# Gated cross-attention and expert FFN on one core: keys projected once, split high and low, and repeated by DMA through a DRAM scratch, with 96-row score operands and a new order of the turn

## What is computed

```python
q, k, v = split_heads(ln(x) @ Wq.T + bq), split_heads(ctx @ Wk.T + bk), split_heads(ctx @ Wv.T + bv)
scores = einsum('bhqd,bhkd->bhqk', q, k) / sqrt(8)
scores = where(mask, finfo.min, scores)
x = x + tanh(g_xattn) * (merge(softmax(scores) @ v) @ Wo.T + bo)
n = ln(x)
w = softmax(n @ Wg + bg) - sigmoid(n @ Wt + bt) / 8, negatives set to 0, normalised over the experts
x = x + tanh(g_ffn) * sum_e w_e * (gelu(n @ W1_e + b1_e) @ W2_e + b2_e)
```

## Time and profile before

| | us |
|---|---|
| median of 3 runs | 683.03 |
| profiled execution, whole | 685.3 |
| its span | 683.5 |
| first T10 (group 0) | 34.20 |
| T10 of group 14 | 265.47 |
| T10 of group 15 | 280.44 |
| last product of the attention phase ends | 297.4 |
| TensorE busy | 633.4 (93%) |
| VectorE busy | 532.4 (78%) |
| ScalarE busy | 432.8 (63%) |
| GpSimd busy | 188.4 (28%) |
| mean granted TensorE clock | 0.98 |

### The profile page before, as it was taken

The page is one execution under the profiler, slowest core; times in us unless marked ns, Lnnn a source line. Parts: engine busy times, 40 slices in busy tenths (PEclk is TensorE's granted clock), DMA queues, the critical chain, the costliest instruction groups (busy, mean ns, idle before and its releaser), DMA issues.

```text
span 683.5 us, 14449 instructions
## 1 busy us (share of the span) xinstructions
PE 633.4 (93%) x3944; PEld 478.2 (70%) x3944; DVE 532.4 (78%) x1083; ACT 432.8 (63%) x764; POOL 188.4 (28%) x242
## 2 busy tenths in 40 slices
PE   2899999999999999739999999999999999999996
PEld 2566666666666766427878878778788788787784
DVE  5778888899988888346877877868778778788686
ACT  3456666666666666418767757667576677675773
POOL 6224444444444443100230221212302202213022
PEclk9999999999999999959999999999999999999999
DMA  6544444444444444103121111111211211111110
GB/s 190 140 110 121 109 120 119 114 114 116 111 111 111 114 110 114 40 0 85 47 62 43 51 47 56 51 34 64 70 35 46 61 46 46 46 61 53 54 46 15
DMA packets 37386, 52.74 MB, mean 77 GB/s; under 512 B 9328, under 2 KB 20464, under 8 KB 37360
## 3 DMA queue, kind: packets, MB, share of 16 engines
q1 hardware_dynamic: 37360, 52.42, 27.8%
HBM read 26.58 MB, written 2.23 MB: 42 GB/s over the span
## 4 chain that ended last, share of the span: by engine, by line
PE 79%; DVE 8%; POOL 3%; DMA 3%; issue 2%; SPq 2%; ACT 2%; DVEq 0%; POOLq 0%; ACTq 0%
PE ps_y L1041 8%; PE ps_y L1043 8%; PE ps_y L1042 8%; PE ps_h L1061 8%; PE ps_h L1063 8%; PE ps_h L1062 8%; PE scores L994 5%; PE scores L995 4%; PE scores L1002 3%; PE scores L1003 3%; POOL yT L527 3%; DVE neg_max L654 3%; PE heads L1013 3%; PE misc L882 2%; PE misc L883 2%
## 5 line engine op out<-in xcount | busy, mean ns | idle before, releaser
L627 ACT ACTIVATE h_sb<-ps_h,b_sb 128x512 f32<-128x512 f32 x256 | 175.4, 689 | 116.2 <-PE ps_h L1063 103.6
L841 DVE TENSOR_TENSOR h_low<-h_sb,h_high 128x512 fp32r<-128x512 f32 x256 | 164.4, 682 | 0.0
L527 POOL TENSOR_TENSOR yT<-yT,weighted 128x512 f32<-128x512 f32 x56 | 72.3, 1292 | 309.2 <-DVE weighted L829 308.4
L837 DVE CAST h_high<-h_sb 128x512 fp32r<-128x512 f32 x128 | 86.8, 678 | 81.8 <-ACT h_sb L627 81.8
L1041 PE MATMUL ps_y<-h_high,w_high 128*128 128x512 f32 x256 | 102.2, 399 | 5.0 <-DVE h_low L841 5.0
L1061 PE MATMUL ps_h<-x_high,w_high 128*128 (+1 forms) x256 | 101.9, 398 | 0.1
L1043 PE MATMUL ps_y<-h_high,w_low 128*128 128x512 f32 x256 | 101.3, 396 | 0.0
L1042 PE MATMUL ps_y<-h_low,w_high 128*128 128x512 f32 x256 | 100.9, 394 | 0.0
L1063 PE MATMUL ps_h<-x_high,w_low 128*128 (+1 forms) x256 | 100.8, 394 | 0.0
L1062 PE MATMUL ps_h<-x_low,w_high 128*128 (+1 forms) x256 | 100.0, 391 | 0.0
L654 DVE TENSOR_REDUCE neg_max<-scores 128x4 f32<-128x512 f32 x128 | 83.6, 685 | 12.5 <-PE scores L1003 11.7
(11 more groups left out here) (122 smaller groups left out, 990.7 us busy)
## 6 DMA issues: line engine op xcount, KB each, us to landing
w_row<-w_scratch SPq DMA_DIRECT2D x64, 256.0 KB, 3.2
k_masked<-k_stack SPq DMA_DIRECT2D x64, 128.0 KB, 2.4
k_cur<-k_stack SPq DMA_DIRECT2D x16, 512.0 KB, 3.0
q_masked<-q_stack SPq DMA_DIRECT2D x64, 96.0 KB
w_raw<-in_w_ffn SPq DMA_DIRECT2D x16, 256.0 KB, 2.7
ctx_sb<-in_ctx SPq DMA_DIRECT2D x16, 128.0 KB, 2.1
out_y<-y_out SPq DMA_DIRECT2D x8, 256.0 KB, 3.6
probs<-in_wqk SPq DMA_DIRECT2D x2, 256.0 KB, 3.1
```

What stands on the lines that cost most here:

```text
L527: nc.gpsimd.tensor_tensor(yT[:], yT[:], weighted[:, e % 2, :], ALU.add).then_inc(added, 1)
L627: nc.scalar.activation(h_sb[:, j % HBUF, :], ps_h[:, j % 4, :], ACT.Gelu_apprx_tanh, bias=b1_sb[:, j:j + 1]).then_inc(h_done, 1)
L841: V.tensor_tensor(h_low[:, j % HBUF, :], h_sb[:, j % HBUF, :], h_high[:, j % HBUF, :].bitcast(F32), ALU.subtract).then_inc(low2_done, 1)
```

## The change

- Keys are projected once: three matmuls with 128 output rows, dense weights `wk_high` and `wk_low`. ScalarE adds the bias and rounds to `k_high`, VectorE leaves the rest in `k_low`. SyncE stores `k_high` twice and `k_low` once to a DRAM scratch `k_scratch` of 96 rows a group (`store`), and from there loads `k_cur` (96 rows, one DMA) and `k_masked` (four DMAs of 24 rows). `k_stack` goes, with four of the eight `part` and `stacks` steps of a turn.
- Queries stay threefold by matmuls, but with 96 instead of 128 output rows. The score operands have 96 rows (98 with the two rows of maxima).
- The pipeline is one turn deeper: inputs are turned in turn it for group it+3 (before it+2), heads, `merged` and `wo` follow one turn later, x2T and gate two turns.
- Biases come by twelve small DMAs that ScalarE issues at the start.
- All engines' orders are written anew. On TensorE `values(g, 0, 0)` and `values(g, 0, 1)` stand apart.

The diff, its core (lines of other moved steps are left out, and `part` and `stacks` of the queries, which only lose rows 96 to 127):

```diff
-BANKS = [["p45", "inputs", "x2T", "p01"],
-         ["p67", "max0", "p23"],
-         ["v", "heads", "merged", "gate", "wo"]]
-AHEAD = {"p45": 1, "p67": 1, "v": 1, "inputs": 2, "x2T": -1, "max0": 1, "heads": 0,
-         "p01": 2, "merged": 0, "p23": 2, "gate": -1, "wo": 0}
-FIRST, LAST = -3, NG
-STEADY = (2, NG - 3)
+BANKS = [["k", "x2T", "q01", "inputs"],
+         ["heads", "merged", "wo", "max0", "gate", "q23"],
+         ["v"]]
+AHEAD = {"k": 2, "x2T": -2, "q01": 2, "inputs": 3,
+         "heads": -1, "merged": -1, "wo": -1, "max0": 1, "gate": -2, "q23": 2, "v": 2}
+FIRST, LAST = -4, NG + 1
+STEADY = (2, NG - 4)
+KROWS = 3 * ROWS * HD
...
+        k_dram = nc.dram_tensor("k_scratch", (NG, KROWS, SLABS * GT), F32)
...
-                sp.dma_start(q_masked[24:26, :, :, b * S:(b + 1) * S].rearrange("p r s q -> p (r s) q").bitcast(F32),
+                sp.dma_start(q_masked[KROWS:KROWS + 2, :, :, b * S:(b + 1) * S].rearrange("p r s q -> p (r s) q").bitcast(F32),
                              maxT[:, b * S:(b + 1) * S].bitcast(F32)).then_inc(max_in[b], 16)
+            store_v = k_dram[:].rearrange("g (r c d) (s t) -> g c r (d s) t", r=ROWS, c=3, t=GT)
+            def store(c, src, g, done):
+                sp.dma_start(of_group(store_v, g)[:, c].rearrange("g r p t -> (g r) p t"), src[:].bitcast(F32)).then_inc(done, 16)
+            def load(dst, rows, g):
+                return sp.dma_start(dst.rearrange("p s t -> p (s t)").bitcast(F32), of_group(k_dram[:], g)[:, rows, :].rearrange("g p x -> (g p) x"))
             def body(it):
-                if (g := group_at(it, 0)) is not None:
-                    sp.wait_ge(maxT1_done, g + 1)
-                    settle(sp)
-                    max_rows(1)
-                if (g := group_at(it, 1)) is not None:
-                    misc_wait_read(sp, "p01", it - 1)
-                    settle(sp)
-                    misc_wait_read(sp, "p23", it - 1)
-                    settle(sp)
-                    if isinstance(g, int) and g == 0:
-                        sp.wait_ge(pad_done, 2)
+                if (g := group_at(it, 2)) is not None:
+                    sp.wait_ge(k_high_done, g + 1)
+                    settle(sp)
+                    store(0, k_high, g, high_stored)
+                    store(2, k_high, g, high_stored)
+                    misc_wait_read(sp, "k", g)
+                    settle(sp)
+                    store(1, k_low, g, low_stored)
+                if (g := group_at(it, 1)) is not None:
+                    sp.wait_ge(high_stored, g * 32 + 32)
+                    settle(sp)
+                    sp.wait_ge(low_stored, g * 16 + 16)
+                    settle(sp)
+                    if first(g):
+                        sp.wait_ge(pad_done, 3)
+                    else:
+                        sp.wait_ge(scoresT_full[1], fill_of(g - 1, GB - 1, SLABS - 1))
+                        settle(sp)
+                    load(k_cur[0:KROWS, :, :], slice(0, KROWS), g).then_inc(kcur_in, 16)
+                    misc_wait_read(sp, "q01", g)
+                    settle(sp)
+                    misc_wait_read(sp, "q23", g)
+                    settle(sp)
+                    for r in range(ROWS):
+                        rows = slice(3 * HD * r, 3 * HD * (r + 1))
+                        sp.dma_start(q_masked[rows, r, :, :].bitcast(F32), q_stack[rows, :, :].bitcast(F32)).then_inc(qm_in, 16)
+                    misc_wait_read(sp, "max0", g)
+                    settle(sp)
+                    max_rows(0)
+                if (g := group_at(it, 2)) is not None and not first(g):
+                    sp.wait_ge(masknxt_done, g)
+                    settle(sp)
+                    sp.wait_ge(maskcur_done, g)
+                    settle(sp)
+                    sp.dma_start(mask_words[:], of_group(mask_v, g)).then_inc(mask_in, 16)
+                if (g := group_at(it, 3)) is not None and not first(g):
+                    misc_wait_full(sp, "inputs", g - 1)
+                    settle(sp)
+                    sp.dma_start(ctx_sb[:], of_group(ctx_v, g).rearrange("g p b d -> (g p) b d")).then_inc(ctx_in, 16)
+                if (g := group_at(it, 2)) is not None:
+                    if not first(g):
+                        sp.wait_ge(wsplit_done, g)
+                        settle(sp)
+                        sp.dma_start(w_raw[:], of_group(a["w_ffn"], g).rearrange("g p x -> (g p) x")).then_inc(w_in, 16)
+                    sp.wait_ge(high_stored, g * 32 + 32)
+                    settle(sp)
+                    sp.wait_ge(low_stored, g * 16 + 16)
+                    settle(sp)
+                    if first(g):
+                        sp.wait_ge(pad_done, 3)
                     else:
                         sp.wait_ge(scoresN_full[1], fill_of(g - 1, GB - 1, SLABS - 1))
                         settle(sp)
                     for r in range(ROWS):
-                        rows = slice(32 * r, 32 * r + 32)
-                        sp.dma_start(k_masked[rows, r, :, :].bitcast(F32), k_stack[rows, :, :].bitcast(F32)).then_inc(km_in, 16)
-                if (g := group_at(it, 3)) is not None and not (isinstance(g, int) and g == 0):
-                    misc_wait_full(sp, "inputs", it)
-                    settle(sp)
-                    sp.dma_start(ctx_sb[:], ctx_v[g] if isinstance(g, int) else ctx_v[bass.ds(g, 1)]).then_inc(ctx_in, 16)
-                if (g := group_at(it, 1)) is not None:
-                    misc_wait_read(sp, "p45", it)
-                    settle(sp)
-                    misc_wait_read(sp, "p67", it)
-                    settle(sp)
-                    if not (isinstance(g, int) and g == 0):
-                        sp.wait_ge(scoresT_full[1], fill_of(g - 1, GB - 1, SLABS - 1))
-                        settle(sp)
-                    for r in range(ROWS):
-                        rows = slice(32 * r, 32 * r + 24)
-                        sp.dma_start(q_masked[rows, r, :, :].bitcast(F32), q_stack[rows, :, :].bitcast(F32)).then_inc(qm_in, 16)
-                    sp.dma_start(k_cur[:].bitcast(F32), k_stack[:].bitcast(F32)).then_inc(kcur_in, 16)
-                    misc_wait_read(sp, "max0", it)
-                    settle(sp)
-                    max_rows(0)
-                if (g := group_at(it, 2)) is not None and not (isinstance(g, int) and g == 0):
-                    sp.wait_ge(masknxt_done, g)
-                    settle(sp)
-                    sp.wait_ge(maskcur_done, g)
-                    settle(sp)
-                    sp.dma_start(mask_words[:], mask_v[g] if isinstance(g, int) else mask_v[bass.ds(g, 1)]).then_inc(mask_in, 16)
-                    sp.wait_ge(wsplit_done, g)
-                    settle(sp)
-                    sp.dma_start(w_raw[:], a["w_ffn"][g] if isinstance(g, int) else a["w_ffn"][bass.ds(g, 1)]).then_inc(w_in, 16)
+                        rows = slice(3 * HD * r, 3 * HD * (r + 1))
+                        load(k_masked[rows, r, :, :], rows, g).then_inc(km_in, 16)
+                if (g := group_at(it, 1)) is not None:
+                    sp.wait_ge(maxT1_done, g + 1)
+                    settle(sp)
+                    max_rows(1)
             loop(sp, body)
...
+            bias_v = a["bqk"].rearrange("(r c d) (n s) -> n r c d s", r=ROWS, c=COMBOS, s=SLABS)
+            for r in range(ROWS):
+                rows = slice(3 * HD * r, 3 * HD * (r + 1))
+                act.dma_start(bk[4 * HD * r:4 * HD * (r + 1), :], bias_v[0, r, 0]).then_inc(bias_in, 16)
+                act.dma_start(bq[rows, :], bias_v[1, r, 0:3].rearrange("c d s -> (c d) s")).then_inc(bias_in, 16)
+                act.dma_start(low_rows[rows, :], a["low_rows"][4 * HD * r:4 * HD * r + 3 * HD, SLABS:]).then_inc(bias_in, 16)
...
+                    misc_wait_full(act, "k", g)
+                    wait_count(act, high_stored, g * 32)
+                    nc.scalar.activation(k_high[:], misc[:, bank_of("k"), 0:GT], ACT.Identity, bias=bk[:]).then_inc(k_high_done, 1)
...
-                    k = bank_of(f"p{i}{i + 1}")
-                    dve.wait_ge(part_done, g * (2 * SLABS) + (i + 2))
-                    if i < SLABS:
-                        wait_count(dve, km_in, g * (ROWS * 16))
-                        wait_count(dve, kcur_in, g * 16)
-                    else:
-                        wait_count(dve, qm_in, g * (ROWS * 16))
-                    for j in (i, i + 1):
-                        dst = (k_stack if j < SLABS else q_stack)[:, j % SLABS, :]
-                        ins = nc.vector.scalar_tensor_tensor(dst, misc[:, k, (j - i) * GT:(j - i + 1) * GT], bqk[:, j:j + 1],
-                                                             part[:, j % 4, :].bitcast(F32), ALU.add, ALU.subtract)
-                    ins.then_inc(misc_read[k], 1)
-                if (g := group_at(it, 1)) is not None:
-                    stacks(2, g)
+                    what = f"q{i}{i + 1}"
+                    dve.wait_ge(part_done, g * SLABS + (i + 2))
```

(23 more changed lines are left out.)

502 lines of the change are left out of this document (264 added, 238 removed).

## The result

| | us |
|---|---|
| kernel before, median of 5 runs | 683.03 |
| changed kernel, median of 5 runs (688.07 to 691.30) | 690.13 |
| ratio, with its 95% interval | 1.0095 (1.0074 to 1.0115) |
| changed kernel, profiled execution, whole | 690.13 |
| its span | 688.4 |

The account below looks back on a forecast made before the run. TensorE sets the turn before the change (16.32 us); after it, SyncE's loop of 17.09 us was to decide. Start +4.9, middle +7.3, end -1.4 sum to +10.8: 694 us against 683.03, 1.6% slower, range 679 to 702.

Parts of the forecast that it names:

- the middle: Attention phase, T10 of group 0 to group 14: 14 turns of 17.09 us, 238.6 against 231.27, +7.3 us.
- a loop over SyncE: Steady turn: T10, T13, SyncE's issues from `k_cur` to `max_rows(1)`, its landing, next T10; one trip is 17.09 us.
- T13 to the issue of `k_cur`: Steady turn: from T13's start on TensorE to SyncE's first issue behind it, 0.92 us.
- `k_cur` to `max_rows(1)`, issuing: Steady turn: SyncE's issues and waits from `k_cur` until `max_rows(1)` is issued, 10.82 us.
- landing of `max_rows(1)`: Steady turn: from the start of its issue until the transfer that T10 needs has landed, 2.26 us.
- the price of the four loads from DRAM: SyncE's issue time for the four `k_masked` loads of 24 rows: 3.14 us, as for `q_masked` of the same shape.
- The stores cost nothing: Steady turn: stores fall between `max_rows(1)` and T13, with some 5 us there, so they cost nothing.
- TensorE at 15.5: TensorE's need in a steady turn after the change: 16.32 - 1.59 + 0.45 + 0.36 = 15.5 us.
- The start: Up to T10 of group 0: later ScalarE, stores and N00 at 24.8 move it from 34.20 to 39.1, +4.9 us.
- The end: T10 of group 14 to group 15: no `k_masked` load in the way, 13.6 against 14.97, -1.4 us.
- Rival 1: Steady turn: four DRAM loads cost 1.6, loop falls to 15.55, TensorE stays the bound; 669 us; chance 0.18.
- Rival 3: Steady turn: `max_rows(1)` lands after 3.0 us in place of 2.26, 15 turns add 11 us; 705 us; chance 0.08.

## Why the prediction was right, and where it was not

**Sign and range: right. Cause: wrong.** It placed +7.3 of +10.8 in the middle, as a loop over SyncE. The middle gave 1.3 back, and the loss was made before T10 of group 0.

**The loop, term by term.** It exists. Its terms, in turns at whose end T10 waits for `max_rows(1)` (of the changed kernel from 109.06, of the run with the SBUF source from 159.55):

| term | forecast | changed kernel | SBUF source |
|---|---|---|---|
| T13 to the issue of `k_cur` | 0.92 | 1.27 | 1.03 |
| `k_cur` to `max_rows(1)`, issuing | 10.82 | 9.42 | 10.57 |
| landing of `max_rows(1)` | 2.26 | 3.21 | 2.40 |
| T10 to T13 | 3.09 | 2.81 | 2.95 |
| together | 17.09 | 16.71 | 16.95 |

With the forecast's price the forecast's loop comes out, each term within 0.3 us. At the real price it sets only some turns: in the shown turn of 16.14 its landing found room, and TensorE's work and the gate's wait set the time.

The step that failed is the price of the four loads from DRAM: 3.14 was taken because "shape is what the rows differ by" (they differ by source too), 1.81 was measured, and the run with an SBUF source shows 3.08 at the same shape. The same error, smaller, is in `k_cur`: 0.53 against 0.34. The row that said so was there: `w_raw`, from DRAM, was the cheapest of the loads, and I put that down to its 128 rows. The Trainium skill ("DMA: Bandwidth & Descriptors", on why a DMA increments its semaphore by 16) was leaned on for the high price, since it has the sequencer write the increments of engines left out; by that the two loads of 24 rows would cost alike. The runs don't agree: 0.33 and 0.72 us by source (medians of 64 issues each).

**"The stores cost nothing": wrong, and this was the change's real cost.** In issuing they push `k_cur` by up to 0.24 us: it follows T13 by 1.04 where the store of `k_low` is issued half a us ahead of T13 (144.88 and 145.42, `k_cur` at 146.46), and by 1.27 or 1.28 where it is issued just behind T13. In the queues they run at a share of 0.23, and what stands behind them lands later (`k_cur` 5.6 against 3.6). The same section of the Trainium skill states the rule that I should have put against the change: the number of engines is the largest up to 16 that divides the slowest dimension of both sides, 4 for these stores, and "Rules for kernel authors" on the same page advises a multiple of 16 outermost. The traces agree with it as far as a share can: 0.23 with 4 outermost, 0.39 and twice the GB/s with 32. I used the rule for the loads and did not try it on the stores.

**TensorE at 15.5.** It was 15.62 busy, which bears the work of the sum out, and 0.44 of the gate's wait for the bank that it shares with the maxima. The wait was in the new order of the turn and I had not looked for one there. The 96- and 98-row operands take the 0.46 us a pair that was taken for them (T13 at 161.53 to its `natural` at 161.99).

**The start: +4.9, and it was +7.76.** ScalarE's first work came 1.58 late (9.13 against 7.55) and not 1.0; the store landed after 5.50 and not 3.6, the row that I took it from being a store of another form; so N00 came at 26.70 and not 24.8. The other 1.0 came behind N00, and not on the path forecast: T10 of group 0 did not wait for `k_cur` and SyncE's issues up to `max_rows(1)`. The chain ran over the maxima to `max_rows(0)`, issued at 33.48, its landing of 3.97 where 2.26 was taken, and TensorE's 4.26 from T00 to T10.

**The end: -1.4, and it was -0.71.** Right in kind.

**The rivals.** Rival 1 had the price right (1.81, under its 2.4) and the time wrong by 21 us, since it took TensorE's 15.5 as free of waits and the landings as before. The row set against it (3.14 for issues, 2.44 for a landing) compares four issues with one transfer: a single issue of 0.79 is a third of that landing. Rival 3, late landing, is what happened, though in the start and the first turns and with the stores as the cause; in later turns it was late too where T10 waited (3.21), and cheaper issues paid for it. In the profiled executions the forecast was off by -8.6 us in the middle, +2.9 at the start, +0.7 at the end and -0.9 behind it. That it came within 4 us of the measured median, and inside its range, is partly luck: errors of both signs cancelled, and the cause named was not the one that cost the time.

## What to carry to other kernels

Look at the slowest dimension of both sides of every DMA that is added: with 4 outermost the stores here ran at a DMA share of 0.23, and what was queued behind them landed late, so the delay showed up at other transfers. Price an issue by its source as well as by its shape, and give each load that is moved its due time before it is moved. Where two resources bind within half a us of each other, as here, relieving one can give nothing until the other is found too.

## What was not expected of the hardware

- Issue time on SyncE of a DMA of 24 rows x 4 KB into SBUF: 0.33 us from DRAM and 0.72 from SBUF, with the same destination and bytes (medians of 64).
- Three stores with 4 as the slowest dimension: 63 GB/s and a DMA share of 0.23 while they run, and 5.50 us for one at the start; with 32: 132 GB/s, 0.39 and 3.15 us. A load of 384 KB behind them landed in 5.6 and in 3.6 (medians of 16).
- The granted clock was lower in stretches in which TensorE waited some us: 0.83 from 50 to 60 us after the change (TensorE busy for 8.18 of 10), with 0.50 from 54 to 56 behind two us of which it worked 0.51, and 0.91 over the turns with a wait of 3 us for ctx; it was 1.00 in the steady turns. In group 1 the lower level took about 1.5 us between T00 and T10 (6.23 us against 4.98 less a wait of 0.21 at 1.00), nearly as much as the wait of 1.82 ahead of T00.
